# One float32 product per step of a recurrence, the gate's bias inside the tanh, and the decay as a scaled copy with a scan over three elements per batch

## The reference, cut to what matters

```
Wh, Wz = W[:, :D], W[:, D:]
leak = 1.0 - alpha
def step(h, z_t):
    gate = sigmoid(h @ Wh.T + z_t @ Wz.T + b)
    h_new = tanh(h * leak + gate * z_t)
    return h_new, h_new
_, hs = scan(step, h_0, z)      # h_0 = cond_1024, z = x after layer 1, 256 steps
x = x + hs
```

## Time and profile before

| | us |
|---|---|
| median of 3 runs | 520.59 |
| profiled execution | 519.57 |
| its span, first to last instruction | 517.8 |
| PE busy in it | 464.6 (90%) |
| DVE busy | 355.4 (69%) |
| ACT busy | 273.0 (53%) |
| POOL busy | 30.7 (6%) |
| mean granted TensorE clock | 0.968 of full speed |

### The profile page before, as it was taken

How to read it: one execution, slowest core, us unless ns; L and a number is a source line. 1 busy time by engine, 2 the same in 40 slices (tenths; PEclk the granted TensorE clock), 3 DMA queues, 4 the chain that set the end, 5 groups by cost and what they waited for, 6 DMA issues and landing times. The chain is left out here.

```text
span 517.8 us, 12688 instructions
## 1 busy us (share of the span) xinstructions
PE 464.6 (90%) x4202; PEld 312.7 (60%) x4202; DVE 355.4 (69%) x1562; ACT 273.0 (53%) x1112; POOL 30.7 (6%) x108
## 2 busy tenths in 40 slices
PE   3899997888999998999998878899998799999995
PEld 2667576556676676766765335566564566766662
DVE  5766887887887888778777688877533865555501
ACT  3442644644646546455455754465668544454561
POOL 7120100000200101010000000000000000000000
PEclk9999997998999999999999978999999799999997
DMA  8400000000000000000000000000000000000000
GB/s 313 187 1 1 2 0 3 2 1 2 1 2 3 1 1 3 1 2 2 1 2 2 0 1 1 3 1 3 1 22 3 1 22 3 1 1 23 2 3 21
DMA packets 4912, 8.30 MB, mean 16 GB/s; under 512 B 496, under 2 KB 3824, under 8 KB 4720
## 3 DMA queue, kind: packets, MB, share of 16 engines
q1 hardware_dynamic: 4416, 7.23, 3.9%
q10 hardware_dynamic: 432, 0.27, 0.2%
HBM read 6.44 MB, written 1.05 MB: 14 GB/s over the span
## 5 line engine op out<-in xcount | busy, mean ns | idle before, releaser
L822 PE MATMUL ybk<-hg,down 128*128 128x256 f32 x352 | 97.5, 401 | 2.0 <-DVE hg L1160 1.2
L968 PE MATMUL hid<-xsp,up 128*128 128x256 f16 x672 | 94.5, 281 | 3.9 <-DVE up L1046 1.6
L734 ACT ACTIVATE d<-cbk 128x8 f32<-128x8 f32 x256 | 45.8, 179 | 96.9 <-PE cbk L990 95.7
L1283 DVE TENSOR_TENSOR_SCAN vbk<-d 128x16 f32<-128x16 f32 x256 | 51.2, 200 | 34.7 <-ACT d L734 31.4
L746 ACT ACTIVATE hhi<-vbk 128x8 f16<-128x8 f32 x255 | 44.9, 176 | 53.3 <-DVE vbk L1283 52.9
L987 PEld LDWEIGHTS cbk<-hhi,wh 128*128 128x128 f16 x512 | 38.0, 99 | 54.5 <-ACT hhi L746 45.1
L968 PEld LDWEIGHTS hid<-xsp,up 128*128 128x128 f16 x672 | 60.6, 100 | 14.2 <-ACT hb L674 2.2
L822 PEld LDWEIGHTS ybk<-hg,down 128*128 128x128 f32 x352 | 60.6, 192 | 8.9 <-DVE hg L1160 2.1
L1201 DVE TENSOR_REDUCE wm<-hid 128x2 f32<-128x256 f32 (+2 forms) x94 | 50.7, 541 | 22.0 <-PE hid L881 19.8
L987 PE MATMUL cbk<-hhi,wh 128*128 128x8 f16 x512 | 51.3, 171 | 11.1 <-ACT hhi L746 9.4
L1270 DVE TENSOR_TENSOR hlo<-hs,hhi 128x8 f16<-128x8 f32 x255 | 42.8, 168 | 24.4 <-ACT hs L747 21.2
(11 more groups left out here) (212 smaller groups left out, 716.1 us busy)
## 6 DMA issues: line engine op xcount, KB each, us to landing
qz<-up_in SPq DMA_DIRECT2D x3, 512.0 KB, 7.8
kp<-maskr_in SPq DMA_DIRECT2D x1, 1024.0 KB, 11.8
out_dram<-silu SPq DMA_DIRECT2D x4, 256.0 KB, 2.3
x<-x_in SPq DMA_DIRECT2D x7, 128.0 KB, 8.8
down<-down_in SPq DMA_DIRECT2D x1, 768.0 KB, 9.8
att<-att_in SPq DMA_DIRECT2D x1, 751.0 KB, 9.9
down<-down_in SPq DMA_DIRECT2D x1, 640.0 KB, 6.9
qz<-up_in SPq DMA_DIRECT2D x1, 256.0 KB, 3.8
```

The lines of the kernel that those rows point to most:

```text
L734: nc.scalar.activation(d1[:, t % 2, :, 0], cbk[c % 2][:, o:o + B], ACT.Tanh, scale=0.5 / RS).then_inc(gate_th, 1)
L822: m = pe.matmul(ybk[l][:, 0:n], D(l, "w2" if shared else "e2", e * f + i), hg[:, hg_of[made] % NHG, i * n:i * n + n], start=first and i == ...
L968: m = pe.matmul(into, up[:, pw, a:a + P], x_part(c, l, px, slice(0, n)), start=j == 0, stop=j == 2)
L1283: nc.vector.tensor_tensor_scan(vps, d0[:, t % ZR].rearrange("p b o -> p (b o)"), d1[:, t % 2].rearrange("p b o -> p (b o)"), 0.0, ALU.mult ...
```

## The change

A step's three fp16 products become one float32 product of Wh with `hs`. The bias leaves `cbk` (two products a chunk less in `C`) and is added in the gate's tanh, as an operand `hb2` of 128 values. `hhi`, `hlo`, `wh2`, the fp16 bias, the factor RS and the units `WH` go. The decay leak * h is made by ScalarE, as a copy with an operand as its scale, right after the tanh of the new state and behind a wait for that tanh's own semaphore. VectorE loses both small operations of a step. The scan runs over three elements per batch: factors (0, z/2, 1) and addends (tanh, z/2, leak * h). Both lie in one tile `dd`, so `Z` writes z/2 twice (512 elements instead of 256). Two buffers of the attention, `eimg` and `onq`, now lie in tiles of the experts. ScalarE makes the first decay before its first units, after a wait for the constants.

```diff
 plan():
-        add(("C", c), mm4(n) + 2 * n / 2.4, 0, 0, False, (("YE", c, 1), "dve", "pe"), (("WH", 2), "dve", "pe"))
-        if c == 0:
-            for i in range(3):
-                add(("WH", i), 0, 0, 700, False, (("E", 0, 1, 0), "pe", "dve"))
+        add(("C", c), mm4(n), 0, 0, False, (("YE", c, 1), "dve", "pe"))
...
 tiles:
-        d0 = sb("d0", [P, ZR, B, 2])
-        d1 = sb("d1", [P, 2, B, 2])
+        dd = sb("dd", [P, ZR, 2, B, 3])
-        eimg = sb("eimg", [P, 2, 2 * QT])
+        eimg = xsp0[:].rearrange("p a r n -> p (a r n)").bitcast(F32).rearrange("p (a n) -> p a n", a=2)
-        onq = sb("onq", [P, 4, P])
+        onq = sel[:].rearrange("p e n -> p (e n)").bitcast(F32).rearrange("p (a d) -> p a d", d=P)
...
 GpSimd:
-            nc.gpsimd.memset(d0[:], 0.0).then_inc(pool_set, 1)
+            nc.gpsimd.memset(dd[:, :, 0, :, 0], 0.0)
+            nc.gpsimd.memset(dd[:, :, 0, :, 2], 1.0).then_inc(pool_set, 1)
...
 ScalarE:
+            act.wait_ge(consts, 1)
+            nc.scalar.activation(dd[:, 0, 1, :, 2], hs[:, 0, :], ACT.Copy, scale=leak[:, 0:1]).then_inc(decay, 1)
...
-                    nc.scalar.activation(d0[:, z0:z0 + CHUNKS[c], :, 1], x[:, cols(c)].rearrange("p (t b) -> p t b", b=B),
-                                         ACT.Copy, scale=0.5).then_inc(act_done, 1)
+                    z = x[:, cols(c)].rearrange("p (t o b) -> p t o b", o=1, b=B).broadcast_to([P, CHUNKS[c], 2, B])
+                    nc.scalar.activation(dd[:, z0:z0 + CHUNKS[c], :, :, 1], z, ACT.Copy, scale=0.5).then_inc(act_done, 1)
...
-                    nc.scalar.activation(d1[:, t % 2, :, 0], cbk[c % 2][:, o:o + B], ACT.Tanh,
-                                         scale=0.5 / RS).then_inc(gate_th, 1)
+                    nc.scalar.activation(dd[:, t % ZR, 1, :, 0], cbk[c % 2][:, o:o + B], ACT.Tanh,
+                                         bias=hb2[:, 0:1], scale=0.5).then_inc(gate_th, 1)
...
-                    new = vps.rearrange("p (b o) -> p b o", o=2)[:, :, 1]
+                    new = vps.rearrange("p (b o) -> p b o", o=3)[:, :, 2]
+                    nc.scalar.activation(hs[:, t + 1, :], new, ACT.Tanh).then_inc(h_full, 1)
                     if t + 1 < T:
-                        nc.scalar.activation(hhi[:, (t + 1) % 2, :], new, ACT.Tanh).then_inc(h_hi, 1)
-                    nc.scalar.activation(hs[:, t + 1, :], new, ACT.Tanh).then_inc(h_full, 1)
+                        act.wait_ge(h_full, t + 1)
+                        nc.scalar.activation(dd[:, (t + 1) % ZR, 1, :, 2], hs[:, t + 1, :], ACT.Copy,
+                                             scale=leak[:, 0:1]).then_inc(decay, 1)
...
 TensorE:
-                    cb = cbk[c % 2][:, 0:n]
-                    pe.matmul(cb, wz, x[:, cols(c)], start=True, stop=True)
-                    for i in range(2):
-                        m = pe.matmul(cb, id16[:], b2[:, i:i + 1].broadcast_to([P, n]), start=False, stop=True,
-                                      skip_group_check=True)
+                    m = pe.matmul(cbk[c % 2][:, 0:n], wz, x[:, cols(c)], start=True, stop=True)
...
-                        pe.wait_ge(h_hi, t)
-                    for i in (1, 0):
-                        pe.matmul(pre, wh2[:, i, :], hhi[:, t % 2, :], start=False, stop=True, skip_group_check=True)
-                    if t:
-                        pe.wait_ge(h_lo, t)
-                    pe.matmul(pre, wh2[:, 0, :], hlo[:, t % 2, :], start=False, stop=True,
-                              skip_group_check=True).then_inc(gate_pre, 1)
+                        pe.wait_ge(h_full, t)
+                    pe.matmul(pre, wh, hs[:, t, :], start=False, stop=True, skip_group_check=True).then_inc(gate_pre, 1)
...
 VectorE:
+            tsc(hb2[:], S("b2"), 0.5, None, ALU.mult)
...
-                if t:
-                    dve.wait_ge(h_full, t)
-                    tts(hlo[:, t % 2, :], hs[:, t, :], hhi[:, t % 2, :], ALU.subtract).then_inc(h_lo, 1)
-                dve.wait_ge(act_done, nth["act", ("Z", chunk_of(t))])
-                stt(d1[:, t % 2, :, 1], hs[:, t, :], leak[:], d0[:, t % ZR, :, 1], ALU.mult, ALU.add).then_inc(decay, 1)
...
-                nc.vector.tensor_tensor_scan(vps, d0[:, t % ZR].rearrange("p b o -> p (b o)"),
-                                             d1[:, t % 2].rearrange("p b o -> p (b o)"), 0.0, ALU.mult,
+                nc.vector.tensor_tensor_scan(vps, dd[:, t % ZR, 0].rearrange("p b o -> p (b o)"),
+                                             dd[:, t % ZR, 1].rearrange("p b o -> p (b o)"), 0.0, ALU.mult,
                                              ALU.add).then_inc(blend, 1)
```

More of the change, by code:

```diff
@@ L76 @@
 GS = 256.0
-RS = 256.0
 REC, N_REC = columns(("wh", P), ("wz", P))
@@ L274, in plan @@
                 ok = end in step_slot and step_slot[end] + 2 <= s
-            if ok and ("C", 0) not in slot_of and key[0] not in ("W", "WH", "XS", "C", "Z", "X3", "MB"):
+            if ok and ("C", 0) not in slot_of and key[0] not in ("W", "XS", "C", "Z", "X3", "MB"):
                 ok = key[1] <= 1 and ("W", 0, 0) in slot_of
@@ L406, in build @@
         sth, sgl = silu[:, 0], silu[:, 1]
-        wh2 = sb("wh2", [P, 2, P], F16)
-        b2 = sb("b2", [P, 2], F16)
+        hb2 = sb("hb2", [P, 1])
         leak = sb("leak", [P, 1])
         warm = sb("warm", [P, 1])
-        d0 = sb("d0", [P, ZR, B, 2])
-        d1 = sb("d1", [P, 2, B, 2])
+        dd = sb("dd", [P, ZR, 2, B, 3])
         hs = sb("hs", [P, T + 1, B])
-        hhi = sb("hhi", [P, 2, B], F16)
-        hlo = sb("hlo", [P, 2, B], F16)
         x3 = sb("x3", [P, B, T])
@@ L454, in build @@
         hid = [ps(f"hid{i}") for i in range(NHT)] + [vbk] + cbk
-        vps = vbk[:, 0:2 * B]
+        vps = vbk[:, 0:3 * B]
         abk = ybk
@@ L478, in build @@
         blend = sem("blend")
-        h_hi = sem("h_hi")
         h_full = sem("h_full")
-        h_lo = sem("h_lo")
         stored = [sem("stored0"), sem("stored1")]
@@ L828, in unit @@
                     pe.wait_ge(dve_done, nth["dve", ("YE", c, 1)])
-                    pe.wait_ge(dve_done, nth["dve", ("WH", 2)])
+                    pe.wait_ge(in_rec, 32)
                     if c >= 2:
                         pe.wait_ge(gate_th, STARTS[c - 1])
-                    cb = cbk[c % 2][:, 0:n]
-                    pe.matmul(cb, wz, x[:, cols(c)], start=True, stop=True)
-                    for i in range(2):
-                        m = pe.matmul(cb, id16[:], b2[:, i:i + 1].broadcast_to([P, n]), start=False, stop=True,
-                                      skip_group_check=True)
+                    m = pe.matmul(cbk[c % 2][:, 0:n], wz, x[:, cols(c)], start=True, stop=True)
                 elif kind in ("KP", "QP"):
@@ L1033, in unit @@
                     hk = hid[bank_of[key]]
-                if kind in ("IK", "VD", "WH", "W") and half != 1 and nth["dve", key] > 1:
+                if kind in ("IK", "VD", "W") and half != 1 and nth["dve", key] > 1:
                     dve.wait_ge(dve_done, nth["dve", key] - 1)
@@ L1046, in unit @@
                     i = stt(up[:, 1, a:b], raw[:, a:b], WS, up[:, 0, a:b], ALU.mult, ALU.subtract)
[L1047 to L1059, removed]
                 elif kind == "IK":
```

## The result

The changed kernel takes 557.44 us (median of 4, 555.14 to 558.73), the one before 522.56 in the same comparison; the ratio is 1.068 (95% interval 1.060 to 1.076). The forecast was 535.5 us, slower by 3%, and the range ended at 547. The direction held, and so did the mechanism of ScalarE's queue; the size did not, and the time lies outside the range. The kernel before is at the high end in this comparison: its medians in the later ones are 519.6 to 520.3 us.

What follows compares the result with a forecast made beforehand. The chain of each step's dependent operations (1.17 us) bounded some steps, TensorE others. Interval terms of +15.2 us on the profiled 519.57 gave 534.8; with the median 1.0 higher it said 535.5 us, forecast 528 to 542, range 516 to 547.

Steps and rivals of the forecast that it cites:

- ScalarE's queue: Behind the decay's copy, late units start at `hs` + 0.355 us and delay the gate: intervals at least 1.39 or 1.49 us.
- the intervals without a late unit: Steps: 92 with TensorE straight from units, 1.25 to 1.29 us, +3.6; 76 where TensorE waits, 1.33 to 1.28, -4.4.
- What would show it: Signs in the later profile: product records 0.11 us apart, gate's tanh 0.26, `E` 0.15 after the copy, TensorE's idle time growing.
- The product, in the chain: From the float32 product's start to the gate: 0.41 us, bounds 0.33 and 0.46; from `hs` 0.64 in all.
- TensorE's place: Time the product holds TensorE where units fill the interval: 0.22 us in place of 0.07, bounds 0.16 and 0.28.
- The tanh with an operand: In the gate, the bias operand lengthens the 8-column tanh by 0.08 us; bounds nothing and 0.10.
- `Z`: Writing 512 elements instead of 256 takes about 0.61 us instead of 0.43, delaying the tanh of 7 steps: +1.4 us.
- VectorE.: Two operations, 0.39 us together, leave each step; VectorE falls to some 260 us busy, idle before nearly every scan.
- The first, an operand that costs nothing at 8 columns: Rival for the gate's tanh: the operand is free, chain 1.11 us, -4 us, 516.5 us; chance 0.10.
- The one with ScalarE passing its own wait at once: Rival for ScalarE: the decay's copy takes 0.15 us all told, late units from `hs` + 0.20; +4 us, 524.5; chance 0.10.
- the last but one, VectorE as the bound: Rival: VectorE's queue held the steps, so relieving it makes the kernel faster, 505 to 512 us; chance 0.12.
- The last (+27 us, TensorE as the bound): Rival: the product holds TensorE 0.28 us and the chain 0.46; +27 us, 547 us; chance 0.10.

Runs made afterwards that it cites:

- both back: The changed kernel with the decay back on VectorE and the bias back in the gate's sum: 517.29 us, ratio 0.994 to the kernel before.
- three fillers: The changed kernel plus three unread products of 256 fp16 columns ahead of TensorE's wait for `hs`, steps 184 to 231: 552.27 us, ratio 1.061.
- five: The changed kernel plus five unread filler products ahead of TensorE's wait for `hs`, steps 176 to 239: 557.19 us, ratio 1.070.

## Why the prediction was wrong in size

What each part costs, by the medians:

| part | added to the kernel before | taken from the changed kernel |
|---|---|---|
| operand in the tanh | +18.0 | -18.5 |
| copy on ScalarE, wait and place | +19.2 | -21.0 |
| float32 product | -8.3 | +8.4 |
| wider scan, double z/2 | +6.0 (both back, against the product alone; 1 to 6, see there) | |

The first column adds up to 34.9 us, against 34.9 in the first comparison and 37 to 38 by the other runs of the kernel before. Each value has an interval of some 3 us to either side, so the agreement is partly luck. The step intervals of the profiled executions are finer, in us:

| change of the intervals | steps 0 to 176 | 176 to 240 | 240 to 255 |
|---|---|---|---|
| operand alone | +12.3 | +4.9 | +1.0 |
| copy alone | +7.5 | +8.5 | +2.1 |
| product alone | -9.6 | +0.6 | +0.2 |
| wider scan, double z/2 | +4.3 | -1.6 | +0.2 |
| sum of the four | +14.5 | +12.4 | +3.5 |
| the changed kernel | +16.2 | +18.4 | +2.7 |

The parts add up to within 2 us but for steps 176 to 240, where the changed kernel loses 6 us more than they do; 4.6 of these are the product's, which costs 0.6 there alone and 5.2 in the changed kernel.

Against the list of the forecast's sum, sorted in the same way (what stands behind the new state in ScalarE's queue), in us:

| intervals | forecast | measured |
|---|---|---|
| 52 with an `E` | +9.4 | +14.5 |
| 20 with an `S` (21 now) | +4.6 | +7.5 |
| 15 with `K` or `Q` | +2.3 | +4.7 |
| 168 without a late unit (167 now), `Z` and bias in them | -1.1 | +10.7 |

The sum gave +15.2 and the intervals show +37.3: 22 us are missing, 10.4 in the first three lines and 11.8 in the last.

- **The step that failed first: the intervals without a late unit, put at about nothing.** In steps 0 to 176 that was right: these intervals took 159.3 us before and 159.4 now, and the product's gain and the operand's cost cancel there, as forecast (-8.6 and +8.2 us in the runs with one of them alone). In steps 176 to 240 they take 58.7 us in place of 48.6, which is most of this line's miss. TensorE ran at 1.2 GHz for 55 of these steps' 104 us, for 10 of 86 before. The chain is 1.42 us at that level, with 0.63 of it the product's way to the gate, units take twice their time (products of 256 fp16 columns follow one another by 213 ns in place of 109), and intervals of 2.0 to 2.5 us appear. I took every duration from rows at 2.4 GHz, and wrote in "What would show it" only that TensorE's idle time would grow, without asking what its clock would do then. How much of the 10 us is the clock is only in part shown: three fillers gave 4.8 us of these steps back, and five gave back nothing net.
- **The step that failed second: the term of ScalarE's queue, right in mechanism and too small.** The copy starts 0.21 us after `hs` (0.20 forecast), but lasts 0.30 and holds the queue 0.21 (0.15 forecast). The interval with `E` is 1.44 at the least (1.39), with `S` 1.53 (1.49). The 52 intervals with `E` average 1.51 (1.41 forecast). Half of that difference is the copy's place. The other half is a slip of the sum: the average was 0.07 above the shortest before and is so now, but the forecast's 1.41 lies only 0.02 above its own 1.39, although it says that the delays are kept in. What the lines of `S`, `K` and `Q` lack (5.3 us) lies mostly in steps 176 to 240 again, and is not parted from the clock.
- **The product, in the chain: right.** 0.41 us forecast, 0.43 measured at 2.4 GHz. **TensorE's place: a little dear.** 0.22 was forecast. Of the 84 steps at full clock in which TensorE waited for nothing, the next instruction started 0.14 us behind the product in 32 and 0.18 to 0.32 behind it in 41. Where it is 0.14 the product's second record starts 0.03 us after the first; after a wait it is 0.13.
- **The tanh with an operand: right.** 0.08 forecast, 0.09 measured (270 ns against 179 before): at 8 columns it costs as much as at 512 (87 ns by rows 8). "The shorter product is eaten by the operand" was right, too. But it hid a choice: the product without the operand is 8 us faster than the kernel before.
- **`Z`: too small.** 0.61 us forecast, 0.89 measured for 512 elements written three elements apart:

```profile
L621 ACT ACTIVATE dd<-x 128x512 f32<-128x512 f32 x8 | 7.1, 887 | 7.0 <-DVE x L1145 7.0
```

- **VectorE.** Its load fell, but to 296 us busy, not 260: the removed operations overlap in the trace with what stands beside them, by some 0.08 us, and without them the kernel before has 295.7 us of busy time. As forecast it was idle ahead of most scans, and that was worth little.
- **The forecast's own signs** came in kind: after a wait the two records are 0.13 us apart (0.11) and the gate 0.43 us after the first, its tanh takes 0.27, there is no idle time ahead of the gate behind an `E`, and TensorE is idle for 68 us in place of 53. `E` starts 0.21 us behind the copy (0.15). A small slip: 534.8 and 1.0 us make 535.8, not 535.5.
- **The rivals.** The first, an operand that costs nothing at 8 columns, is refuted by the 0.09 us and the 18 us of the operand alone. The one with ScalarE passing its own wait at once (+4 us) is refuted by 0.21 us between `hs` and copy, and the last but one, VectorE as the bound, by 211 scans that wait for the gate. The last (+27 us, TensorE as the bound) came nearest in size, but not in mechanism: the product's place is 0.14 to 0.27 us in most steps and not 0.28, its way 0.43 and not 0.46, and by itself it makes the kernel faster.

## What to carry to other kernels

In a loop of short operations, price each part by itself before setting one against another: here two parts of the change lost 18 and 19 us and hid a third that gains 8. Their sum held to within 2 us where the granted clock stayed as it was, and fell 6 us short in the steps where it did not. An operation put on an engine that also carries long units costs its place, its operand and the wait for its input in every round in which a long unit stands behind it: place it behind the long unit (15 us back here), or on an engine with time to spare (21 back). And where a change makes TensorE wait more, ask what the granted clock will do.

## What the runs showed that I had not expected

- An 8-column copy on ScalarE with an operand as scale takes 304 ns and holds its queue for 0.19 to 0.21 us; a tanh without operand holds it for 0.05 to 0.07.
- Waiting for the own engine's last result costs 0.14 us of queue (0.21 against 0.05 to 0.07 from start to start), some 10.6 us over the 255 steps.
- A float32 product of 8 columns needs 0.43 us from its start to its reader's at 2.4 GHz and 0.63 at 1.2 GHz.
- The same product gains 9.4 us over steps 0 to 176 of the changed kernel and costs 5.2 over steps 176 to 240, where TensorE is at 1.2 GHz for half the time.
- The scan over 24 elements takes 217 ns, the one over 16 took 200: 2.1 ns per element. This agrees with the half throughput of the Trainium skill's page on DVE opcodes ("DVE: opcode table, instruction layouts, handler registers and perf-mode slots", section 6), if one element at full rate takes the 1.05 ns of VectorE's wide operations (L1165 of the kernel before: 416 ns for 256 elements, 686 for 512).
